# The first routing of a macaron block: a shorter product chain, earlier row stores, later expert weights, and another source of ones

## The chip, the cores and the metric

The kernel runs on one core of a Trainium2 chip. The metric is the device time of one execution in microseconds (us). The core has five engines that work beside each other and meet only at semaphores: TensorE (PE, matrix products and transposes), VectorE (DVE), ScalarE (ACT), GpSimd (POOL) and SyncE (SP, which here only issues transfers). Transfers are carried out by 16 DMA engines, whichever engine issued them. TensorE's clock has two levels, 2.4 and 1.2 GHz; the profile gives the granted clock as a share of the higher one.

## The reference

The input x is 4 batches of 512 tokens with 128 values each. The reference computes a "macaron" block of three residual steps:

```
x = x + 0.5 * ffn(layernorm(x))          # 8 experts, each token goes to one (top 1)
x = x + attention_block(layernorm(x))    # linear attention, then a quantised feed-forward net
x = x + 0.5 * ffn(layernorm(x))          # the same 8 experts again

def ffn(x):                              # W1: 8 x 128 x 512, W2: 8 x 512 x 128
    probs = softmax(x @ router_W + router_b)
    top1  = argmax(probs)
    h = relu(x @ W1[e] + b1[e]); y = h @ W2[e] + b2[e]
    return probs[top1] * y[top1]
```

The change lies in the first of the three steps, and in one preparation for the third.

## The kernel before

**Tiling.** The 2,048 tokens are 16 tiles of 128 rows, four to a batch. The first step sorts tokens by expert: every token gets a rank within its expert, every expert gets whole tiles of 128 slots, and 23 tiles (NT) are enough for any routing. The normalised rows are written to a scratch tensor in HBM (xn_scratch). For each slot tile the kernel gathers 128 rows from there by an indirect transfer, loads the expert's first weights and biases, and does the two layers. The second expert layer reads its weights W2 directly from the buffer that holds all eight experts.

**First routing.** Each engine has its own program.
- SyncE issues the loads of x (four), the router bias, the expert biases, all of W1 (2 MB), and then W2 of five experts (`load_w2`, five loads of 256 KB, in 512-byte pieces). Then it waits for the list of tile codes (`whole_ready`), reads it, and issues the loads of each tile's weights; from the second tile on it waits for the first gather too.
- VectorE makes the means and variances batch by batch. It then picks each token's expert in two halves (`pick(0, 0, 2)` and `pick(0, 2, 2)`, L1330), and between these makes a shift (minus mean times reciprocal deviation, `first_shift`) for each batch. The shift of batch 3 comes after the second pick. Then `route` (L1381) copies the hits, takes the tile counts, the ranks, the tile codes, and writes the source list srcu for the gathers.
- GpSimd makes constants in a fixed order, each raising `const_ready` by one: 7 is the step selectors, 8 the step column add_step, 9 rowid, 10 tileid, 11 and 12 token numbers, 13 and 14 the head masks. Among them it makes the reciprocal deviations (`first_rstd`). After 12 it writes all four tiles of batch 2's normalised rows (L582), then three tiles of row hits, then the masks, and a few small fills. Then it waits for the four row stores and for srcu and issues the gathers (L610). During gathers 10 to 13 it also fills xn with ones, a quarter at a time.
- ScalarE copies the transposed rows, writes the normalised rows of batches 0, 1 and 3 (`renormalise`, L775, each waits for its shift), and stores all four batches (`store_xn`, L782), batch 2 last, since GpSimd writes that one. Later it loads W2 of the last three experts.
- TensorE transposes x, makes the logits, and then in `ranks` (L977) and `tile_list` (L1011) the ranks and the tile table, as sums of products with masks. Products that are done only to keep the clock up are called warm products (`keep_warm(n)`, L927: each 512 columns of bf16). After the first routing's `sources` come eleven of them, and then the experts.

**Third step.** Its rows go to another scratch tensor, row_scratch, which has to hold ones wherever no token lands. SyncE fills it during attention: it waits until xn is full of ones (`fill_ready`) and until the last rows of the first step are back, then writes 9.2 MB from xn in nine transfers, each raising `fill_done`. GpSimd waits for `fill_done` before it scatters rows there. The buffer actT holds the looked-up activations of two batches; its half 1 is first written by the look-up of batch 1 (`lookup`, L861) on ScalarE.

Of the kernel before, what the change touches and what calls it, by code (L numbers as in the profile page):

```python
# [5 lines left out]
P = 128  # L6
D = 128
B = 4
S = 512
TOK = B * S  # L10
T = TOK // P
# [27 lines left out]
FILL = CODES * P * PW // P  # L39
UNROLL = 8  # L40
# [6 lines left out]
FILL_AT, FILL_PARTS = 10, 4  # L47
ROWS_BY_ACT = 4
ROWS_BY_POOL = 3
POOL_ROWS = 2  # L50
W2_BY_ACT = 3
# [14 lines left out]
def macaron_kernel(nc, x_d, g1_d, b1_d, wq_d, wk_d, wv_d, wo_d, g2_d, b2_d, w1_d, w2_d,  # L66
# [18 lines left out]
    with ctx:  # L85
        def sb(name, shape, dt=f32):
            return ctx.enter_context(nc.sbuf_tensor(name, shape, dt))
# [113 lines left out]
        actT = sb("actT", [P, 2, FC, S])  # L201

# [199 lines left out]
        def _(sp):  # L402
# [5 lines left out]
            sp.dma_start(ew[:, :, W1_AT:W1_AT + F], ew1_d.rearrange("e p f -> p e f")).then_inc(ew_in, 16)  # L408
            load_w2(sp, range(NE - W2_BY_ACT))
# [33 lines left out]
            sp.wait_ge(fill_ready, FILL_PARTS)  # L443
            sp.wait_ge(yb_in[NG - 1], 16 * GT)
            for at in range(0, FILL, T * D):
                n = min(T * D, FILL - at)
                sp.dma_start(row_fill_v[:, at:at + n], xn[:, :, :].rearrange("p t d -> p (t d)")[:, 0:n]).then_inc(fill_done, 16)
# [25 lines left out]
        def _(pool):  # L473
# [92 lines left out]
            step_selectors()  # L566
# [4 lines left out]
            at.then_inc(const_ready, 1)  # L571
            g.iota(rowid[:, :], [[1, P]], base=0, channel_multiplier=0,
# [7 lines left out]

            for t in range(POOL_ROWS * GT, (POOL_ROWS + 1) * GT):
                last = g.tensor_scalar(xn[:, t, :], x[:, t, :], mv[:, t, 0:1], rstd[:, t, 0:1], ALU.subtract, ALU.mult)  # L582
            last.then_inc(xn_by_pool, 1)

# [5 lines left out]
            for m_, pat in ((bmask[:, :, :], [[-DH, H], [0, DH]]), (hmask[:, :], [[-DH, H]])):  # L590
                link(g.affine_select(out=m_, in_=m_, compare_op=ALU.is_ge, fill=0.0, base=0,
                                     pattern=pat, channel_multiplier=1))
                g.affine_select(out=m_, in_=m_, compare_op=ALU.is_ge, fill=0.0, base=DH - 1,
                                pattern=[[-s_, n_] for s_, n_ in pat], channel_multiplier=-1).then_inc(const_ready, 1)
# [3 lines left out]
            g.memset(vx[:, :, :, D:D + 1], 1.0).then_inc(ones_ready, 1)  # L598

# [7 lines left out]
            def move_rows():  # L607

                def gather(k):
                    g.indirect_dma_start(out=Xg[:, k % UNROLL, :], out_offset=None, in_=xn_scr,  # L610
                                         in_offset=bass.IndirectOffsetOnAxis(ap=srcu[:, k:k + 1], axis=0)
                                         ).then_inc(g_in[k % UNROLL], 16)

                for b in range(NG):
                    pool.wait_ge(xn_stored[b], 16)
                pool.wait_ge(src_ready, 1)
                for k in range(NT):
                    if k >= UNPACED:
                        paced(k - UNPACED)
                    gather(k)  # L620
                    if FILL_AT <= k < FILL_AT + FILL_PARTS:
                        ts = slice((k - FILL_AT) * GT, (k - FILL_AT + 1) * GT)
                        g.memset(xn[:, ts, :], 1.0).then_inc(fill_ready, 1)
                pool.wait_ge(posu_ready, 1)
# [82 lines left out]
            pool.wait_ge(fill_done, 16 * len(range(0, FILL, T * D)))  # L707
# [9 lines left out]
        def _(act):  # L717
# [57 lines left out]
            def renormalise(g):  # L775

                act.wait_ge(shift_ready, g + 1)
                for t in range(g * GT, (g + 1) * GT):
                    last = A(xn[:, t, :], x[:, t, :], ACT.Identity, scale=rstd[:, t, 0:1], bias=shift[:, t, 0:1])
                last.then_inc(xn_ready, 1)  # L780

            def store_xn(g):  # L782
                if g == POOL_ROWS:
                    act.wait_ge(xn_by_pool, 1)
                else:
                    act.wait_ge(xn_ready, 1 + g - (g > POOL_ROWS))
                act.dma_start(xn_scr_v[:, g, :, :], xn[:, g * GT:(g + 1) * GT, :]).then_inc(xn_stored[g], 16)
# [22 lines left out]
            store_xn(3)  # L810
            store_xn(POOL_ROWS)
# [49 lines left out]
            def lookup(b, chunks=range(FC)):  # L861
                for c in chunks:
# [58 lines left out]
        def _(pe):  # L921
# [55 lines left out]
            def ranks():  # L977
# [3 lines left out]
                pe.wait_ge(const_ready, 10)  # L981
                mm(bank[5][0:NV, 0:1], whole[:, :], ones_v[0:1, 0:1], start=True, stop=False, skip_group_check=True)
                mm(bank[5][0:NV, 2:4], ident[0:NV, 0:NV], add_step[:, :], start=False, stop=False, skip_group_check=True)
# [10 lines left out]
                keep_warm(1)  # L994
# [3 lines left out]
                mm(bank[6][:, 0:NT], ones_v[0:1, :], tileid[0:1, :], start=True, stop=False, skip_group_check=True)  # L998
# [12 lines left out]
            def tile_list():  # L1011

                pe.wait_ge(tcol_ready, 1)
# [4 lines left out]
                keep_warm(1)  # L1018
# [136 lines left out]
            keep_warm(11)  # L1155
# [149 lines left out]
        def _(dve):  # L1305
# [63 lines left out]
            def first_shift(g):  # L1369

                ts = slice(g * GT, (g + 1) * GT)
                dve.wait_ge(rstd_ready, g + 1)
# [217 lines left out]
            first_shift(2)  # L1590
# [4 lines left out]
            first_shift(3)  # L1595
# [175 lines left out]
```

## Time and profile before

| | us |
|---|---|
| median of 3 runs | 207.23 |
| lowest, highest | 206.13, 208.17 |
| the profiled execution's own time | 205.5 |
| its span, first to last instruction | 203.8 |

| engine | busy us | share of the span |
|---|---|---|
| PE matmul | 187.3 | 92% |
| PE weight load | 158.8 | 78% |
| DVE | 122.3 | 60% |
| ACT | 111.8 | 55% |
| POOL | 122.2 | 60% |

The profile is of one execution; starts are counted from the beginning of its span. Busy time on TensorE includes the modelled end of each product and the warm products, so a busy TensorE isn't one that does useful work. L and a number is a line of the kernel. In a timeline a row may stand for several like instructions (x4), and the brackets at its end give the idle time before it and what ended that. "issue" is time in which the engine waited for nothing that the profile shows. The run is about 1.7 us longer than the span.

### The profile page before, as it was taken

To read this page: it belongs to the slowest core of one execution; us is meant where nothing else is said; L and a number is where in the kernel's file an instruction comes from. 1 tells how busy PE (TensorE), PEld (TensorE's weight loads), DVE (VectorE), ACT (ScalarE), POOL (GpSimd) and SP (SyncE) were. 2 spreads that over 40 slices of the span, in tenths; PEclk is the share of its full clock that TensorE was granted. 3 is DMA by queue.
4 is the path that set the end of the run, shared out by engine and by line. 5 is a ranking of instruction groups with operands and counts; after the bars stand their busy time and mean duration, and the time that the engine had idled before them with its cause. 6 is when DMAs were issued, how large, how long until landed. Compare 5 with 4: busy or idle time off the path is not lost.

```text
span 203.8 us, 4562 instructions
## 1 busy us (share of the span) xinstructions
PE 187.3 (92%) x1410; PEld 158.8 (78%) x1410; DVE 122.3 (60%) x518; ACT 111.8 (55%) x326; POOL 122.2 (60%) x186
## 2 busy tenths in 40 slices
PE   4999769999999978998999999989998999999992
PEld 2985349899999966786865869679635999999991
DVE  4767511222222887898897584867515677777762
ACT  2457225566556648787969853401302766766770
POOL 6886675697773676371787540847771344544554
PEclk9965599999999999999999999999999999999998
DMA  5999759867798561399991000011037868674800
GB/s 200 226 378 357 252 185 375 286 213 245 204 199 296 140 177 45 132 413 428 413 411 52 2 3 0 30 42 44 30 122 247 286 237 281 225 266 156 274 28 0
DMA packets 26680, 40.26 MB, mean 198 GB/s; under 512 B 4229, under 2 KB 16296, under 8 KB 25632
## 3 DMA queue, kind: packets, MB, share of 16 engines
q1 hardware_dynamic: 21136, 33.01, 46.1%
q0 software_dynamic: 2496, 4.76, 9.1%
q10 hardware_dynamic: 3024, 2.20, 3.4%
q8 instruction: 12, 0.20, 0.4%
q14 instruction: 12, 0.10, 0.1%
HBM read 10.78 MB, written 14.46 MB: 124 GB/s over the span
## 4 chain that ended last, share of the span: by engine, by line
PE 67%; DVE 11%; DMA 10%; issue 4%; POOL 3%; ACT 2%; ACTq 1%; SPq 0%; POOLq 0%; DVEq 0%
PE bank L1102 18%; PE bank L1119 17%; PE bank L1238 7%; PE bank L1254 6%; DMA Xg<-xn_scratch,srcu 4%; PE bank L927 3%; PE bank L974 3%; PE bank L1095 3%; DMA xn_scratch<-xn 2%; DMA eqrq<-row_scratch 2%; PE bank L943 2%; PE bank L1179 2%; DMA w<-in_L_attn_w_dram 2%; PE bank L1193 2%; PE bank L1203 1%
## 5 line engine op out<-in xcount | busy, mean ns | idle before, releaser
L748 ACT ACTIVATE hT<-bank,ewc_own 128x128 f32<-128x128 f32 x184 | 52.5, 369 | 48.3 <-PE bank L1102 48.2
L1102 PE MATMUL bank<-xT,ewc_own 128*128 128x128 f32 x368 | 48.8, 276 | 0.4 <-DVE xT L1455 0.3
L1119 PE MATMUL bank<-ew,hT 128*128 x368 | 48.5, 275 | 0.0
L1102 PEld LDWEIGHTS bank<-xT,ewc_own 128*128 128x128 f32 x368 | 44.7, 192 | 1.2 <-issue 1.2
L1119 PEld LDWEIGHTS bank<-ew,hT 128*128 128x128 f32 x368 | 44.7, 192 | 0.2 <-issue 0.2
L682 POOL DMA_INDIRECT out_dram<-ysb,eqrq x23 | 22.6, 983 | 25.4 <-DVE ysb L1465 25.1
L610 POOL DMA_INDIRECT Xg<-xn_scratch,srcu x23 | 22.0, 958 | 10.6 <-issue 5.8
L927 PE MATMUL bank<-ones_bf 128*128 128x512 bf16 x66 | 21.1, 451 | 3.9 <-POOL ident L500 2.7
L674 POOL DMA_INDIRECT row_scratch<-pay,posu x16 | 15.8, 988 | 10.8 <-DVE posu L1428 7.1
L1461 DVE TENSOR_TENSOR ysb<-bank,ewc_own 128x128 f32<-128x128 f32 x23 | 6.7, 289 | 26.0 <-PE bank L1119 26.0
L635 POOL DMA_INDIRECT xnT<-slot_scratch,posu x16 | 15.9, 997 | 9.4 <-DMA slot_scratch<-ysb 3.1
L1455 DVE COPY xT<-bank 128x128 f32<-128x128 f32 x46 | 13.0, 283 | 7.0 <-PE bank L1095 7.0
L1254 PE MATMUL bank<-w,actT 128*128 128x128 f32 x128 | 16.3, 278 | 0.0
L927 PEld LDWEIGHTS bank<-ones_bf 128*128 128x128 bf16 x66 | 6.8, 114 | 11.2 <-issue 4.3
L1095 PE MATMUL bank<-ident,Xg 128*128 128x128 f32 x46 | 12.9, 281 | 2.7 <-DMA Xg<-xn_scratch,srcu 1.9
L1254 PEld LDWEIGHTS bank<-w,actT 128*128 128x128 f32 x128 | 15.1, 192 | 0.0
L1238 PE MATMUL bank<-h1T,w 128*128 128x512 f32 x32 | 14.4, 592 | 0.0
L1465 DVE SCALAR_TENSOR_TENSOR ysb<-bank,gate,ysb 128x128 f32<-128x128 f32 x23 | 8.1, 351 | 10.3 <-PE bank L1119 10.1
L864 ACT ACTIVATE actT<-ewc_own 128x512 f32<-128x512 int16 x16 | 9.3, 621 | 8.0 <-DVE ewc_own L1666 8.0
L1474 DVE TENSOR_SCALAR Xg<-eqrq 128x128 f32<-128x128 f32 x23 | 7.8, 340 | 4.8 <-DMA eqrq<-row_scratch 4.6
L1238 PEld LDWEIGHTS bank<-h1T,w 128*128 128x128 f32 x32 | 5.8, 190 | 5.7 <-issue 5.5
L1666 DVE TENSOR_SCALAR ewc_own<-bank 128x512 int16<-128x512 f32 x16 | 10.0, 682 | 0.1
(240 smaller groups left out, 305.8 us busy)
## 6 DMA issues: line engine op xcount, KB each, us to landing
ewc_own<-ew SPq DMA_DIRECT2D x46, 322.0 KB, 3.1
row_scratch<-xn SPq DMA_DIRECT2D x8, 1024.0 KB, 10.6
ew<-in_L_ffn_W_dram SPq DMA_DIRECT2D x1, 2048.0 KB, 10.8
slot_scratch<-ysb SPq DMA_DIRECT2D x23, 64.0 KB, 1.8
ew<-in_L_ffn_W_dram SPq DMA_DIRECT2D x5, 256.0 KB, 8.7
eqrq<-row_scratch SPq DMA_DIRECT2D x18, 70.0 KB, 2.4
x<-in_L_attn_x_dram SPq DMA_DIRECT2D x4, 256.0 KB, 3.5
xn_scratch<-xn ACTq DMA_DIRECT2D x4, 256.0 KB, 5.7
```

What stands on the lines that cost most here:

```text
L610: g.indirect_dma_start(out=Xg[:, k % UNROLL, :], out_offset=None, in_=xn_scr, in_offset=bass.IndirectOffsetOnAxis(ap=srcu[:, k:k + 1], axis=0)
L635: g.indirect_dma_start(out=Yg[:, t, :], out_offset=None, in_=slot_scr[0:UPTO[group] * P, :], in_offset=bass.IndirectOffsetOnAxis(ap=posu[: ...
L674: g.indirect_dma_start(out=row_scr, out_offset=bass.IndirectOffsetOnAxis(ap=posu1[:, t:t + 1], axis=0), in_=pay[:, t, :], in_offset=None). ...
L682: g.indirect_dma_start(out=out_rows, in_=ysb[:, k, :], in_offset=None, bounds_check=TOK - 1, oob_is_err=False, out_offset=bass.IndirectOff ...
L748: last = A(hT[:, t.slot, c * P:(c + 1) * P], up_bank(k, c)[:, c * P:(c + 1) * P], ACT.Relu, scale=0.5 if m else 1.0, bias=ewc[t.ahead][:, ...
L927: mm(bank[2][:, :], ones_bf[:, :], bc(ones_bf[:, :].unsqueeze(1), [P, 4, P]), start=True, stop=True)
L1095: nc.tensor.transpose(bank[t.parity][:, 0:P], Xg[:, t.ahead, :], ident[:, :]).then_inc(xg_T, 1)
L1102: last = mm(up_bank(k, c)[:, c * P:(c + 1) * P], ewc[t.ahead][:, c * P:(c + 1) * P], xT[:, t.slot, :], start=True, stop=True)
L1119: last = mm(bank[4 + t.parity][:, 0:D], hT[:, t.slot, c * P:(c + 1) * P], ew[:, bass.ds(e[k], 1), W2_AT + c * D:W2_AT + (c + 1) * D].squee ...
L1238: mm(hidden_bank(c)[:, :], w1[:, c * P:(c + 1) * P], h1T[:, b % 2, :], start=True, stop=True).then_inc(u_ps, 1)
L1254: last = mm(row_bank(b, j)[:, j * P:(j + 1) * P], actT[:, b % 2, c, j * P:(j + 1) * P], w2[:, c, :], start=c == 0, stop=c == FC - 1)
L1455: v.tensor_copy(xT[:, t.slot, :], bank[t.parity][:, 0:P]).then_inc(xT_ready, 1)
```

## The change

- `ranks` waits for six constants where it waited for ten. The product that starts the step columns with add_step stands behind the wait for the second pick, where the product with the tile numbers stood; the latter moves into `tile_list`, in place of a warm product. The warm product in `ranks` is taken out. The eleven warm products before the experts are seven.
- GpSimd writes two of batch 2's four row tiles, before the remaining constants; ScalarE writes the other two. add_step comes before the step selectors (so it is 7 and they are 8). The head masks come before the row hits.
- The shifts of batches 2 and 3 are one VectorE instruction, between the picks.
- SyncE waits until ScalarE has written the rows of three batches (`xn_ready`, 3) before it issues W2's five loads.
- The ones for row_scratch are in a buffer of their own, 128 rows of 512 values that lie in the last quarter of actT's half 1; each transfer reads them repeatedly. There are ten transfers in place of nine. The fills of xn between the gathers are gone, one fill stands before the gathers, and ScalarE waits for `fill_done` before the look-up of batch 1.

```diff
 # SyncE
+            sp.wait_ge(xn_ready, NG - 1)
             load_w2(sp, range(NE - W2_BY_ACT))
 ...
-            sp.wait_ge(fill_ready, FILL_PARTS)
+            sp.wait_ge(fill_ready, 1)
             sp.wait_ge(yb_in[NG - 1], 16 * GT)
             for at in range(0, FILL, T * D):
                 n = min(T * D, FILL - at)
-                sp.dma_start(row_fill_v[:, at:at + n], xn[:, :, :].rearrange("p t d -> p (t d)")[:, 0:n]).then_inc(fill_done, 16)
+                whole_cols = n // FILL_COLS * FILL_COLS
+                sp.dma_start(row_fill_v[:, at:at + whole_cols].rearrange("p (a c) -> p a c", c=FILL_COLS),
+                             bc(filler.unsqueeze(1), [P, n // FILL_COLS, FILL_COLS])).then_inc(fill_done, 16)
+                if whole_cols < n:
+                    sp.dma_start(row_fill_v[:, at + whole_cols:at + n], filler[:, 0:n - whole_cols]).then_inc(fill_done, 16)
 # GpSimd
             for n in range(NG):
                 first_rstd(n)
-            step_selectors()
+            pool.wait_ge(rstd_ready, POOL_ROWS + 1)
+            for t in range(POOL_ROWS * GT + HALF_ROWS, (POOL_ROWS + 1) * GT):
+                last = g.tensor_scalar(xn[:, t, :], x[:, t, :], mv[:, t, 0:1], rstd[:, t, 0:1], ALU.subtract, ALU.mult)
+            last.then_inc(xn_by_pool, 1)
 ...                                  (add_step, const_ready 7)
+            step_selectors()
 ...                                  (rowid, tileid, the token numbers; the four rows stood here;
 ...                                  the head masks now stand here, then the row hits)
             g.memset(vx[:, :, :, D:D + 1], 1.0).then_inc(ones_ready, 1)
+            g.memset(filler, 1.0).then_inc(fill_ready, 1)
 ...
                     gather(k)
-                    if FILL_AT <= k < FILL_AT + FILL_PARTS:
-                        ts = slice((k - FILL_AT) * GT, (k - FILL_AT + 1) * GT)
-                        g.memset(xn[:, ts, :], 1.0).then_inc(fill_ready, 1)
 # ScalarE
-                act.wait_ge(shift_ready, g + 1)
-                for t in range(g * GT, (g + 1) * GT):
+                act.wait_ge(shift_ready, min(g, POOL_ROWS) + 1)
+                for t in range(g * GT, g * GT + HALF_ROWS if g == POOL_ROWS else (g + 1) * GT):
 ...
             store_xn(3)
+            renormalise(POOL_ROWS)
             store_xn(POOL_ROWS)
 ...
             def lookup(b, chunks=range(FC)):
+                if b == 1 and chunks[0] == 0:
+                    act.wait_ge(fill_done, 16 * FILLS)
 # TensorE
                 pe.wait_ge(oh_ready, picks(0, 0))
-                pe.wait_ge(const_ready, 10)
-                mm(bank[5][0:NV, 0:1], whole[:, :], ones_v[0:1, 0:1], start=True, stop=False, skip_group_check=True)
-                mm(bank[5][0:NV, 2:4], ident[0:NV, 0:NV], add_step[:, :], start=False, stop=False, skip_group_check=True)
+                pe.wait_ge(const_ready, 6)
 ...
-                keep_warm(1)
+                mm(bank[5][0:NV, 0:1], whole[:, :], ones_v[0:1, 0:1], start=True, stop=False, skip_group_check=True)
                 pe.wait_ge(oh_ready, picks(0))
                 mm(bank[4][:, 4:5], oh[:, :, :].rearrange("p t e -> p (t e)"), ones_bf[:, 0:1], start=True, stop=True
                    ).then_inc(hits_ps, 1)
-                mm(bank[6][:, 0:NT], ones_v[0:1, :], tileid[0:1, :], start=True, stop=False, skip_group_check=True)
+                pe.wait_ge(const_ready, 7)
+                mm(bank[5][0:NV, 2:4], ident[0:NV, 0:NV], add_step[:, :], start=False, stop=False, skip_group_check=True)
 ...                                  (in tile_list)
+                pe.wait_ge(const_ready, 8)
                 pe.wait_ge(tcol_ready, 1)
 ...
-                keep_warm(1)
+                pe.wait_ge(const_ready, 10)
+                mm(bank[6][:, 0:NT], ones_v[0:1, :], tileid[0:1, :], start=True, stop=False, skip_group_check=True)
                 pe.wait_ge(inv_ready, 1)
 ...
-            keep_warm(11)
+            keep_warm(7)
 # VectorE
             pick(0, 0, 2)
-            first_shift(2)
+            first_shift(2, 2)
 ...
             pick(0, 2, 2)
-            first_shift(3)
```

## Rows read from the trace of the kernel before

**Rows 1.** Chain of waits, 10 to 40 us; start us, us, what.

```profile
17.69 4.64 DMA xn_scratch<-xn
...
23.75 1.25 POOL Xg L610
...
26.55 3.30 DMA Xg<-xn_scratch,srcu
...
30.23 0.92 PE bank L1102 x8
...
31.88 4.33 DMA Xg<-xn_scratch,srcu
```

**Rows 2.** Timeline of VectorE: start, us, line, operation, out<-in, shapes [idle before].

```profile
13.56 0.23 DVE L1337 TENSOR_TENSOR lg<-bank,rstd 128x64 f32<-128x64 f32 x1 [0.87 <-PE bank L974]
...
14.33 0.43 DVE L1343 TENSOR_TENSOR lg<-lg,lmax 128x64 f32<-128x64 f32 x1
...
15.91 0.16 DVE L1387 COPY hits<-bank 128x1 f32<-128x1 f32 x1 [0.30 <-PE bank L996]
...
22.50 0.18 DVE L1379 TENSOR_SCALAR srcu<-bank 128x23 uint32<-128x23 f32 x1 [1.09 <-PE bank L1077]
```

**Rows 3.** Timeline of TensorE's products, 10 to 30 us.

```profile
10.63 2.89 PE L974 MATMUL bank<-rwc,xnT 128*128 128x8 f32 x16
...
13.58 0.24 PE L983 MATMUL bank<-add_step,ident 32*32 32x2 f32 x2
...
15.71 0.61 PE L998 MATMUL bank<-tileid,ones_v 1*128 1x23 f32 x2
...
16.50 0.27 PE L1005 MATMUL bank<-hits,sums 128*32 128x1 f32 x2
...
17.31 0.61 PE L927 MATMUL bank<-ones_bf 128*128 128x512 bf16 x1
...
18.46 2.31 PE L927 MATMUL bank<-ones_bf 128*128 128x512 bf16 x5
...
22.31 3.88 PE L927 MATMUL bank<-ones_bf 128*128 128x512 bf16 x11
26.52 0.33 PE L1095 MATMUL bank<-ident,Xg 128*128 128x128 f32 x1 [0.33 <-DMA Xg<-xn_scratch,srcu]
...
29.90 0.33 PE L1095 MATMUL bank<-ident,Xg 128*128 128x128 f32 x1 [1.14 <-DMA Xg<-xn_scratch,srcu]
```

**Rows 4.** Timeline of GpSimd: rows, row hits, and a fill between the gathers.

```profile
13.44 3.14 POOL L582 TENSOR_SCALAR xn<-x,mv,rstd 128x128 f32<-128x128 f32 x4
18.45 2.49 POOL L587 TENSOR_SCALAR inr<-rowid,rf,token 128x128 f16<-128x128 f16 x3 [1.88 <-DVE rf L1402]
...
40.41 0.54 POOL L623 MEMSET xn<- 128x512 f32 x1
```

**Rows 5.** Timeline of ScalarE: the rows of batch 3.

```profile
15.64 1.65 ACT L779 ACTIVATE xn<-x,shift,rstd 128x128 f32<-128x128 f32 x4 [2.42 <-DVE shift L1373]
```

**Rows 6.** Timeline of SyncE's queue, 4 to 33 us.

```profile
4.72 10.11 SPq L371 DMA_DIRECT2D ew<-in_L_ffn_W_dram  x5
21.51 11.10 SPq L417 DMA_DIRECT2D ewc_own<-ew  x8
```

**Rows 7.** Stretches: length, busy us (instructions) by engine, granted clock, DMA share, GB/s.

```profile
11.00:12.00 1.00, 1.00 (x9) 1.00 (x8) 0.90 (x4) 1.00 (x4) 0.68 (x3) 0.71 1.04 401
...
20.00:25.00 5.00, 3.90 (x25) 1.47 (x24) 3.42 (x13) 1.41 (x4) 3.60 (x10) 0.50 0.87 279
25.00:30.00 5.00, 3.20 (x18) 1.66 (x16) 0.58 (x2) 1.14 (x4) 3.79 (x4) 0.99 0.50 172
```

**Rows 8.** Timeline of SyncE's queue: the writes of row_scratch.

```profile
84.56 9.56 SPq L447 DMA_DIRECT2D row_scratch<-xn  x9
```

**Rows 9.** Stretches: the end of these writes.

```profile
105.00:110.00 5.00, 4.75 (x24) 3.03 (x23) 3.60 (x9) 4.67 (x10) 4.57 (x10) 1.00 0.52 214
```

**Rows 10.** Timeline of ScalarE: the first look-ups of batch 1.

```profile
115.21 1.13 ACT L864 ACTIVATE actT<-ewc_own 128x512 f32<-128x512 int16 x2
```

More of the change, by code:

```diff
@@ L39 @@
 FILL = CODES * P * PW // P
+FILL_COLS = S
+FILLS = FILL // (T * D) + (FILL % (T * D) >= FILL_COLS) + (FILL % FILL_COLS > 0)
 UNROLL = 8
@@ L46 @@
 DEEP = 4
-FILL_AT, FILL_PARTS = 10, 4
 ROWS_BY_ACT = 4
@@ L50 @@
 POOL_ROWS = 2
+HALF_ROWS = GT // 2
 W2_BY_ACT = 3
@@ L201, in macaron_kernel @@
         actT = sb("actT", [P, 2, FC, S])
+        filler = actT[:, 1, FC - 1, :]
         ewc = [ewc_own[:, u, :] for u in range(UNROLL)]
@@ L579, in _ @@
                    channel_multiplier=-GT, allow_small_or_imprecise_dtypes=True).then_inc(const_ready, 1)
-            for t in range(POOL_ROWS * GT, (POOL_ROWS + 1) * GT):
-                last = g.tensor_scalar(xn[:, t, :], x[:, t, :], mv[:, t, 0:1], rstd[:, t, 0:1], ALU.subtract, ALU.mult)
-            last.then_inc(xn_by_pool, 1)
-            pool.wait_ge(rf_ready, 1)
-            for t in range(T - ROWS_BY_ACT - ROWS_BY_POOL, T - ROWS_BY_ACT):
-                g.tensor_scalar(inr[:, t, :], rowid[:, :], rf[:, t:t + 1], token1[:, t:t + 1], ALU.is_equal, ALU.mult
-                                ).then_inc(inr_by_pool, 1)
             for m_, pat in ((bmask[:, :, :], [[-DH, H], [0, DH]]), (hmask[:, :], [[-DH, H]])):
@@ L594, in _ @@
                                 pattern=[[-s_, n_] for s_, n_ in pat], channel_multiplier=-1).then_inc(const_ready, 1)
+            pool.wait_ge(rf_ready, 1)
+            for t in range(T - ROWS_BY_ACT - ROWS_BY_POOL, T - ROWS_BY_ACT):
+                g.tensor_scalar(inr[:, t, :], rowid[:, :], rf[:, t:t + 1], token1[:, t:t + 1], ALU.is_equal, ALU.mult
+                                ).then_inc(inr_by_pool, 1)
             g.memset(pay[:, :, TOK_AT + 1:LG_AT], 0.0).then_inc(pay_ready, 1)
@@ L706, in _ @@
             residuals(B - 1)
-            pool.wait_ge(fill_done, 16 * len(range(0, FILL, T * D)))
+            pool.wait_ge(fill_done, 16 * FILLS)
             for b in range(1, B):
@@ L784, in store_xn @@
                     act.wait_ge(xn_by_pool, 1)
-                else:
-                    act.wait_ge(xn_ready, 1 + g - (g > POOL_ROWS))
+                act.wait_ge(xn_ready, (1, 2, 4, 3)[g])
                 act.dma_start(xn_scr_v[:, g, :, :], xn[:, g * GT:(g + 1) * GT, :]).then_inc(xn_stored[g], 16)
@@ L1367, in row_hits, with first_shift @@
                                     ALU.is_equal, ALU.mult).then_inc(inr_ready, 1)
-            def first_shift(g):
-                ts = slice(g * GT, (g + 1) * GT)
-                dve.wait_ge(rstd_ready, g + 1)
+            def first_shift(g, n=1):
+                ts = slice(g * GT, (g + n) * GT)
+                dve.wait_ge(rstd_ready, g + n)
                 v.scalar_tensor_tensor(out=shift[:, ts, 0:1], in0=rstd[:, ts, 0:1], scalar=-1.0, in1=mv[:, ts, 0:1],
```

## The prediction

> **What bounds the kernel now.** I read the chain of waits first. Between the first routing and the first expert it leaves the engines: the store of a batch's normalised rows is under way from 17.69 us for 4.64 us, so lands at 22.33, and GpSimd's first gather begins at 23.75 [rows 1]. Then I read VectorE's timeline for the other thing that the gather waits for: the source list, written at 22.50 in 0.18 us, so there at 22.68 [rows 2]. The two releasers lie 0.35 us apart, and the later one is the list. Whatever frees the stores alone is worth nothing in this execution; what moves the list is worth its full length until the stores are last.
>
> TensorE's timeline shows what the list hangs on and what cover there is. The 16 logits products hold the engine from 10.63 to 13.52. The hits product goes once the last pick is done, then the tile-number product at 15.71 takes 0.61, and only at 16.50 comes the count product, for which everything in VectorE's routing waits [rows 3]. VectorE had its copy of the hits at 15.91 + 0.16 = 16.07 [rows 2]: TensorE, not VectorE, is late there. The first expert's rows are turned at 26.52, and at 29.90, after 1.14 us of idle time, the third tile's [rows 3]. From there TensorE runs with few gaps, so a shift at the third gather goes through to the end, save what a later wait eats.
>
> **The change part by part.**
>
> *Products moved in the ranks.* The tile-number product (0.61) leaves the stretch between hits and counts, and the step product (0.24) comes in [rows 3]. 0.61 - 0.24 = 0.37 us. The count product would start at 16.13, just behind the hits copy's end at 16.07, so no more than 0.43 can be had here, and 0.37 is taken. The tile-number product now stands where a warm product of the same 0.61 stood, at 17.31: nothing. The warm product taken out of the ranks lay before the wait for the second pick: nothing. The waits for constants themselves cost nothing before: logits held the engine until 13.52 and GpSimd had left its constants at 13.44 [rows 4]. All of VectorE's routing, the five warm products at 18.46 [rows 3], TensorE's reading of the list and the source products follow in chain, so the list comes at 22.31.
>
> *GpSimd's order.* Two rows instead of four are written, and before the constants rather than after: 3.14 / 4 = 0.79 each, so the constants end at 13.44 + 1.57 = 15.01 at the latest [rows 4]. The first that is awaited after a pick is needed at about 15.7, the tile numbers at 16.9: 0.7 us of cover or more. The masks move ahead of the row hits; they and the small fills filled at most 20.94 to 23.75, 2.81 us, so they end by 17.8, and the row hits are released at 18.45 - 0.37 = 18.08 [rows 4]. Behind the hits (2.49) comes the new fill of ones, 128x512, at 0.54, as the four taken out of the gathers [rows 4]: 18.08 + 2.49 + 0.54 = 21.1, plus the small fills, under the 22.31 of the list. Cover gone, it would cost 0.54. The four fills taken out stood beside a TensorE that had its tiles: nothing.
>
> *Rows and stores on ScalarE.* It sat idle 2.42 us, from 13.22 on, for the last shift before batch 3's four rows at 15.64 (1.65 us, to 17.29) [rows 5]; the store was under way 0.40 later, at 17.69 [rows 1]. The shift of both batches is now made before the second pick. The rows begin at 13.22, or 13.6 behind the issue of the store before them, and are done by 15.3; the store is under way at 15.7 and lands, with the old 4.64 us, at 20.3. Two rows of batch 2 (0.83) and its store follow: under way at about 16.9, landed at 21.6. Worth nothing by itself, since the list is last; it keeps the stores from being last.
>
> *Second weights.* Five loads, which SyncE issued from 4.72 to 14.83 at 2.0 us each [rows 6], wait for three batches of rows, about 15.3. They are beside the last two stores, not behind them: the wait counts rows written, not stores landed. An issue takes 0.4 where the queue is free (the store's) and, in the burst of eight tile loads with waits in it, at most 11.10 / 8 = 1.4 [rows 1, 5, 6]. Five take 2 to 7 us, so SyncE is free at 17.3 to 22.3; behind them it has the list to read and its first tile load, which stood at 21.51. The weights themselves are wanted by the first down product, behind the 0.92 of the second up that begins at 30.23 [rows 1]: cover enough. Price 0, with up to +0.5 if the first tile load comes over a microsecond late.
>
> *The gathers' landings.* The DMA engines now have the second weights to move while the first gather lands. How much that costs no row shows; it is bounded by the nearest landings. The first turn came 2.77 us after its gather's start; the third landed in 3.30, the sixth, in a crowd, in 4.33 [rows 1, 3]. A first landing of 4.33 would be 1.6 later, of which 1.14 is idle time before the third. A third landing of 4.33 would be a straight +1.03. Less traffic could also give up to -0.5. I take 0, since the crowd should be gone by the time of the third.
>
> *Warm products.* Eleven at 22.31 become seven. They take up to 0.46 each at the lower clock (2.31 / 5), so 3.2 us, ending at 25.2, before the first rows at 26.2: nothing, if the clock is kept.
>
> *VectorE beside GpSimd.* One of the second pick's steps took 0.43 at 14.33, where its neighbour took 0.23 [rows 2]. GpSimd then read and wrote rows [rows 4]. The Trainium skill, SBUF — State Buffer, "SBUF: two separate sides", says that a VectorE instruction with two SBUF inputs and a GpSimd one that reads SBUF exclude each other for a whole instruction. By that rule the rows in their new place would hold up the first pick instead, by up to 0.79 a step, and the trace agrees only in part: one step of several was held, by 0.21. Without the rule: the second pick may gain 0.21 and the first may lose it several times over, but VectorE then sat idle for 0.87 us until the logits were out [rows 2]. Price 0, bounds -0.21 and +0.5.
>
> *The fill of the row scratch.* Nine writes become ten, from one row of 512 ones read again and again. Issued from 84.56 [rows 8], they keep the DMA engines full to about 107.6 (share 0.52 of 105 to 110) [rows 9]. ScalarE must now wait for them before the second batch's look-up at 115.21 [rows 10]. Some 7.6 us of cover on 23 of traffic: it would have to run a third slower to matter. Nothing.
>
> **Sum.** The profiled execution took 205.5 us, its span 203.8 and 1.7 around it. 205.5 - 0.37 = 205.1. The median of the runs shown is 207.23, 1.7 above the profiled one, for reasons that no row tells; with that offset kept, **206.8 us**.
>
> **The rivals.**
> - *Stores were late in the other executions* (0.25). With only 0.35 us between stores and list, an execution with slower stores waits for the stores, and the change takes them out of the way by 1.3 to 2 us. Then the median gains its 1.7 of offset in good part too: 207.23 - 0.37 - 1.4 = 205.4. For: the traffic at that point and the runs' spread of 2 us. Against: nothing shows where the spread comes from.
> - *The clock goes* (0.20), the one that ends slower. Place: the end of the seven warm products. The granted clock was 0.50 over 20 to 25 us and 0.99 over 25 to 30; the five products at 18.46 had not raised it, the sources and the eleven had. It fell at 11 to 12 us with TensorE busy throughout [rows 7]. With four products fewer, TensorE does nothing from about 25.2 to 26.2, and the clock may not rise, or may fall before the third tile. The up and the down products of a tile, 0.92 us each at the full clock [rows 1], then take 1.8: the sixth gather waits for an up, +0.9 at once, up to +1.9 and once more if it lasts. 207.23 - 0.37 + 1.5 = 208.4, to 206.9 + 3.8 = 210.7. It decides as soon as the granted clock is 0.5 at 26 us or later. Against: over 25 to 30 TensorE was busy only 3.20 of 5.00 and kept the clock. The Trainium skill (TensorE: Matmul & The Clock Gate, "What's actually happening") has the clock lowered only after a stretch of idleness; by that rule this rival would be nearly nil, and the sum stands. The fall at 11 to 12 with no idle time disagrees, so I keep its chance.
> - *Second weights in the gathers' way* (0.12): the third landing at 4.33, or a late first tile load: 207.23 - 0.37 + 1.0 = 207.9.
> - *The change doesn't do what it says* (0.08): the count product starts no earlier, because the second pick or the step selectors are late. 207.2.
>
> **How the numbers follow.** My forecast has 0.35. About 1%, 2.07 us, is what a measurement of this kernel can tell from no change. Under 205.16 lie half of the first rival and a fifth of the forecast: 0.20. Above 209.3 lie two fifths of the clock rival and a quarter of the crowd (where it delays several landings): 0.11. Within: 0.69. The range takes in the first rival on one side and the clock's single price on the other: 205.0 to 208.9.
>
> **What would show it.** Right: the count product near 16.1; the source list's write near 22.1; GpSimd's first gather near 23.4; row stores landed by 21.5; third turn near 29.5; clock 1.0 from 25 us. Wrong: the first gather still at 23.7 with VectorE's list unmoved; a granted clock of 0.5 after 26 us; a gather that takes over 4 us before the third turn; ScalarE waiting for the fill near 115 us.

## The result, and the profile after

The changed kernel is slower: 207.53 us against 205.98, both medians of 20 runs; ratio 1.0069, 95% interval 1.0045 to 1.0093, so about +1.4 us. The ratio leaves out executions in a slower state, four of the changed kernel's 20, one of them of 273.35 us. I had forecast 206.8 from a median of 207.23, a gain of 0.4. That 207.53 lies in my range of 205.0 to 208.9 is luck: the range was laid around the median of three runs, 207.23, which 20 runs put at 205.98, and the time moved the other way. The profiled execution has a span of 206.5 us, before 203.8.

The chain of waits of the changed kernel, 10 to 45 us (start us, us, what):

```profile
15.99 3.80 DMA xn_scratch<-xn
...
20.11 0.43 POOL actT L608
20.54 1.91 issue
22.45 0.04 POOLq L626
22.49 0.84 issue
23.34 4.46 DMA Xg<-xn_scratch,srcu
...
28.86 2.05 PE bank L1112 x8
...
31.60 1.97 PE bank L1112 x8
33.57 0.89 PE bank L1129 x8
```

Read it against [rows 1]. The first gather starts 0.41 us earlier (23.34, was 23.75), but takes 4.46 us to land. The two first-layer products behind it ("ups", L1112; the second layer's are "downs", L1129) take 2.0 us each, where they took 0.9 to 1.1. The first down starts at 33.57; before, the second up ended at 31.15 and the down followed. The loss is made between 23 and 34 us.

VectorE and TensorE in their timelines, as in [rows 2, 3]:

```profile
11.60 0.25 DVE L1363 TENSOR_TENSOR oh<-key,kmax 128x64 bf16<-128x64 f32 x1
...
15.08 0.16 DVE L1397 COPY hits<-bank 128x1 f32<-128x1 f32 x1 [1.38 <-POOL token L589]
...
21.65 0.18 DVE L1389 TENSOR_SCALAR srcu<-bank 128x23 uint32<-128x23 f32 x1 [1.07 <-PE bank L1087]
```

```profile
13.76 0.19 PE L1003 MATMUL bank<-ones_bf,oh 128*128 128x1 bf16 x1 [1.01 <-DVE oh L1363]
...
15.38 0.24 PE L1013 MATMUL bank<-hits,sums 128*32 128x1 f32 x2 [0.99 <-DVE hits L1397]
...
21.46 3.15 PE L936 MATMUL bank<-ones_bf 128*128 128x512 bf16 x7
27.84 0.47 PE L1105 MATMUL bank<-ident,Xg 128*128 128x128 f32 x1 [3.23 <-DMA Xg<-xn_scratch,srcu]
...
28.86 2.05 PE L1112 MATMUL bank<-xT,ewc_own 128*128 128x128 f32 x8
```

The source list came at 21.83, 0.85 us earlier than before. A part of it is the clock, which was high during the logits in this execution (below). GpSimd had finished its fill at 20.54 and the list was there at 21.83, yet its wait ended at 22.49. The stores were what it waited for: their landings took 3.6 to 6.4 us, and batch 2's, issued at 15.99, with 6.4 lands at 22.4. TensorE then sat idle for 3.23 us before the first turn.

This holds for the kernel before too, and I had read it otherwise. Its chain, and the time from issue to landing of its last two stores (issued at 17.32 and 17.69):

```profile
17.69 4.64 DMA xn_scratch<-xn
22.33 0.10 POOL pay L596
...
22.48 0.38 issue
22.86 0.04 POOLq L616
...
DMA to landing us min/median/max: 4.8/5.0/5.1
```

The 4.64 us end where a small fill of GpSimd's takes over in the chain, not where the store lands. Batch 2's, issued at 17.69, lands 5.1 us later, at 22.8, behind the list of 22.68, and GpSimd's wait ends at 22.86. So the stores were the last already, by some 0.1 us. They now land 0.4 us earlier, and the first gather starts 0.41 us earlier; the list's 0.85 us show nowhere.

VectorE's copy of the hits shows something that I hadn't priced: 1.38 us of idle time, ended by GpSimd's token numbers. TensorE had the hits at 13.95. The constants, now behind two rows, had become the late ones.

Stretches of both kernels, first before, then after (length, busy us by engine, granted clock, DMA share, GB/s):

```profile
14.00:17.00 3.00, 2.65 (x24) 1.89 (x23) 1.74 (x9) 1.35 (x4) 2.57 (x4) 0.50 1.14 344
...
23.00:25.00 2.00, 2.00 (x6) 0.76 (x5) 1.51 (x6) 0.00 (x0) 1.25 (x1) 0.50 0.87 282
25.00:28.00 3.00, 2.34 (x13) 1.08 (x11) 0.29 (x1) 0.00 (x0) 2.09 (x3) 0.99 0.21 61
```

```profile
14.00:17.00 3.00, 1.91 (x20) 1.65 (x19) 1.34 (x7) 1.75 (x5) 2.09 (x10) 0.50 0.85 295
...
23.00:25.00 2.00, 1.61 (x4) 0.30 (x2) 0.69 (x4) 0.00 (x0) 1.37 (x2) 0.50 1.13 310
25.00:28.00 3.00, 0.16 (x1) 0.16 (x2) 0.00 (x0) 0.00 (x0) 2.39 (x3) 0.50 0.29 85
```

Over 14 to 17 us the DMA engines' share is 0.85 where it was 1.14: W1 runs out, and W2, issued from 14.58 on, comes too late. I call this the hole. The work left undone comes back at 23 to 25 us (0.87 becomes 1.13), under the first gather. Over 25 to 28 us TensorE is busy for 0.16 us, and its clock, which stood at 0.99 before, stays at 0.50, the lower of its two levels, until within 30 to 35 us (0.66 there; before 1.00).

### The profile page after: what moved, and what is told of

The parts are those of the page before. It is cut to its first block, busy times and chain, and to the rows that moved or that the text cites. A ratio compares the mean times of both kernels' runs of the same rounds, so it can differ in the third digit from the quotient of the medians.

```text
span 206.5 us, 4550 instructions
## 1 busy us (share of the span) xinstructions
PE 185.6 (90%) x1404; PEld 157.9 (76%) x1404; DVE 122.2 (59%) x517; ACT 112.7 (55%) x328; POOL 119.0 (58%) x181
## 4 chain that ended last, share of the span: by engine, by line
PE 61%; DVE 11%; DMA 10%; POOL 6%; issue 5%; ACT 4%; SPq 1%; ACTq 0%; POOLq 0%; DVEq 0%
PE bank L1112 19%; PE bank L1129 16%; PE bank L1248 7%; PE bank L1264 5%; POOL row_scratch L681 3%; ACT xn L786 3%; PE bank L1105 2%; DMA Xg<-xn_scratch,srcu 2%; DMA ewc_own<-ew 2%; DMA row_scratch<-pay,posu 2%; PE bank L1189 2%; DMA xn_scratch<-xn 2%; DMA w<-in_L_attn_w_dram 2%; PE bank L952 2%; PE bank L1203 2%
## 5 line engine op out<-in xcount | busy, mean ns | idle before, releaser
L1112 PE MATMUL bank<-xT,ewc_own 128*128 128x128 f32 x368 | 50.6, 282 | 1.3 <-DMA ewc_own<-ew 0.9
L1112 PEld LDWEIGHTS bank<-xT,ewc_own 128*128 128x128 f32 x368 | 46.3, 198 | 3.1 <-issue 1.9
L1129 PE MATMUL bank<-ew,hT 128*128 x368 | 48.5, 275 | 0.0
L1129 PEld LDWEIGHTS bank<-ew,hT 128*128 128x128 f32 x368 | 44.8, 192 | 0.2 <-issue 0.2
L936 PE MATMUL bank<-ones_bf 128*128 128x512 bf16 x60 | 19.2, 454 | 3.8 <-POOL ident L509 2.7
L1264 PEld LDWEIGHTS bank<-w,actT 128*128 128x128 f32 x128 | 15.1, 192 | 0.0
L936 PEld LDWEIGHTS bank<-ones_bf 128*128 128x128 bf16 x60 | 6.1, 114 | 10.4 <-issue 3.9
L1105 PEld LDWEIGHTS bank<-ident,Xg 128*128 128x128 f32 x46 | 6.8, 148 | 5.5 <-DMA Xg<-xn_scratch,srcu 4.1
```

The lines of the kernel that those rows point to most:

```text
L936: mm(bank[2][:, :], ones_bf[:, :], bc(ones_bf[:, :].unsqueeze(1), [P, 4, P]), start=True, stop=True)
L1105: nc.tensor.transpose(bank[t.parity][:, 0:P], Xg[:, t.ahead, :], ident[:, :]).then_inc(xg_T, 1)
L1112: last = mm(up_bank(k, c)[:, c * P:(c + 1) * P], ewc[t.ahead][:, c * P:(c + 1) * P], xT[:, t.slot, :], start=True, stop=True)
L1129: last = mm(bank[4 + t.parity][:, 0:D], hT[:, t.slot, c * P:(c + 1) * P], ew[:, bass.ds(e[k], 1), W2_AT + c * D:W2_AT + (c + 1) * D].squee ...
L1264: last = mm(row_bank(b, j)[:, j * P:(j + 1) * P], actT[:, b % 2, c, j * P:(j + 1) * P], w2[:, c, :], start=c == 0, stop=c == FC - 1)
```

## The experiments

A profile is one execution and the ratio rests on many, so the last two columns of the table tell the mechanism and not the size. All ratios are to the kernel before, with 95% intervals. "First gather" is the time from its start to what it released, in the chain, or else from the timelines to the first turn. The column of W2 says how many of the five loads are issued behind SyncE's wait. Three profiles lie at the edge of their runs: e3's and e5's are of the fastest execution (204.06 and 205.11 us), e12's of the slowest (207.50, median 205.76).

| kernel | W2 behind | warm | ratio | first gather us | first down at us |
|---|---|---|---|---|---|
| before | 0 | 11 | 1 | 2.8 | 31.0 |
| changed | 5 | 7 | 1.0069 (1.0045, 1.0093) | 4.5 | 33.4 |
| e1 | 5 | 11 | 1.0085 (1.0044, 1.0126) | 5.2 | 33.9 |
| e9 | 5 | 20 | 1.0058 (1.0020, 1.0096) | 5.1 | 32.6 |
| e2 | 0 | 7 | 1.0040 (1.0004, 1.0076) | 2.8 | 31.8 |
| e11 | 5, wait one batch earlier | 7 | 1.0029 (0.9993, 1.0066) | 3.2 | 31.2 |
| e12 | 5, wait one batch earlier | 11 | 0.9989 (0.9959, 1.0019) | 3.1 | 32.3 |
| e3 | 0 | 11 | 0.9980 (0.9941, 1.0018) | 3.7 | 30.3 |
| e6 | 3 | 11 | 0.9976 (0.9937, 1.0015) | 3.0 | 31.1 |

**e1, e2, e3: undo the warm products, the wait, both.**

```diff
-            keep_warm(7)
+            keep_warm(11)        # e1, e3
-            sp.wait_ge(xn_ready, NG - 1)      # e2, e3
```

> The changed kernel with eleven warm products before the experts, as before, in place of seven. Clock theory (the cost is TensorE's clock, which stayed at the lower level through the first two ups because too few warm products stood before them): the granted clock is 1.0 by the first up, the ups take 0.9 us instead of 2.0, and the ratio to the kernel before falls from 1.007 to 0.998 to 1.002. Traffic theory (the cost is the first gather, which landed 4.5 us after its start because the second weights were moved at that time): the first turn stays near 27.8 us and the ratio stays at 1.005 to 1.009.

> The changed kernel without SyncE's wait: the second weights of five experts are issued at once, as before; seven warm products stay. Traffic theory: the first gather lands in 2.7 us again, the first turn stands near 25.9, and the ratio is 0.996 to 1.000. Clock theory: the gap before the first turn gets shorter, but seven warm products may still not bring the clock, so the ups stay slow in some executions: ratio 1.000 to 1.005.

> Both undone: no wait of SyncE, eleven warm products. What is left of the change is the shorter product chain, the rows split over two engines and the buffer of ones. Clock and traffic theories together: 0.994 to 0.998, since the source list came 0.85 us earlier in the changed kernel. If the cost lay elsewhere (in the buffer of ones or the new wait of ScalarE): 1.004 or more.

In e1 four warm products given back change nothing (1.0085). That alone doesn't clear the clock: it did rise behind them, but was lost again before the first up, so only e9 below tests it.

```profile
21.82 3.91 PE L936 MATMUL bank<-ones_bf 128*128 128x512 bf16 x11
28.31 0.47 PE L1105 MATMUL bank<-ident,Xg 128*128 128x128 f32 x1 [2.59 <-DMA Xg<-xn_scratch,srcu]
28.58 0.63 PE L936 MATMUL bank<-ones_bf 128*128 128x512 bf16 x1
29.33 2.05 PE L1112 MATMUL bank<-xT,ewc_own 128*128 128x128 f32 x8
```

Eleven products in 3.91 us are 0.36 apiece, against 0.46 in [rows 3] at the lower level: the last of them ran high (granted clock 1.00 over 25 to 28 us, 0.51 over 28 to 30). Between them and the up of 2.05 lie 2.59 us of waiting. Its hole is deeper than the changed kernel's (share 0.53 over 14 to 17, as in e9, 0.52), and its first gather slower, 5.2 us against 4.5. e2 takes the wait away: the first gather lands in 2.8 us, and of the 0.69% some 0.3 go. With seven warm products the ups are still slow (2.05 and 2.04), though the gather is not late: seven are too few by themselves. e3 does both and is at 0.998, clear of the changed kernel's 1.0069, so what it undoes is the whole loss. In its profile the up takes 1.13 us, and its span is 202.3:

```profile
26.27 0.33 PE L1104 MATMUL bank<-ident,Xg 128*128 128x128 f32 x1 [1.44 <-DMA Xg<-xn_scratch,srcu]
26.44 0.38 PE L935 MATMUL bank<-ones_bf 128*128 128x512 bf16 x1
27.15 1.13 PE L1111 MATMUL bank<-xT,ewc_own 128*128 128x128 f32 x8 [0.33 <-DVE xT L1464]
```

**e4: seven warm products in the kernel before.**

```diff
-            keep_warm(11)
+            keep_warm(7)
```

> The kernel before with seven warm products in place of eleven, nothing else. Clock theory: four warm products fewer alone lose the clock in some or all executions, ratio 1.003 to 1.010. Traffic theory: the first gather lands as before, so the gap behind seven warm products is short and nothing changes, 0.999 to 1.001.

0.9994 (0.9955 to 1.0032). Its profile lost the clock all the same (ups of 2.05 and 1.68 us, first down at 31.52, 0.56 later than before), and no time shows. So the lost clock alone is worth less than the 1 to 2 us that I gave it. The first up's delay fills idle time that TensorE has anyway before the third turn [rows 3]: the second up starts at 30.01, where it started at 30.06. A later wait takes most of the rest: the sixth turn is at 36.40, before at 36.25.

**e9: enough warm products to bridge the late gather.**

```diff
-            keep_warm(7)
+            keep_warm(20)
```

> The changed kernel with twenty warm products in place of seven, so that TensorE is at work until the late first gather has landed. If the slow ups are the larger part of the loss: clock 1.0 at the first up, the first down near 31.3 instead of 33.4, ratio 0.998 to 1.003. If the late gather is: the ratio stays at 1.005 or more, for the gathers behind it come late as well.

The clock was kept (an up of 1.13 us at 29.66) and the ratio is still 1.0058: with the gather at 5.1 us the first down comes at 32.6. So the larger part of the loss is the late gather. Its chain shows how that reaches the first down:

```profile
23.68 5.06 DMA Xg<-xn_scratch,srcu
28.74 0.02 issue
28.76 0.21 SPq L422
28.97 0.04 issue
29.02 2.52 DMA ewc_own<-ew
31.53 0.04 issue
31.58 1.17 PE bank L1112 x8
```

SyncE waits for the first gather before it loads the second tile's weights, and these take another 2.5 us; the second up waits for them. I had priced the first gather by the turn behind it alone.

**e5 and e10: the product chain alone; the chain undone.**

```diff
 # e5: on the kernel before, the edits of ranks and tile_list, and add_step ahead of step_selectors
 # e10: on e3
-                pe.wait_ge(const_ready, 6)
+                pe.wait_ge(const_ready, 7)
+                mm(bank[5][0:NV, 0:1], whole[:, :], ones_v[0:1, 0:1], ...)
+                mm(bank[5][0:NV, 2:4], ident[0:NV, 0:NV], add_step[:, :], ...)
 ...
+                pe.wait_ge(const_ready, 10)
+                mm(bank[6][:, 0:NT], ones_v[0:1, :], tileid[0:1, :], ...)   # between hits and counts again
```

> The kernel before with the shorter product chain alone (and the step column made before the step selectors, as it needs): no other part of the change. My sum gave it 0.37 us: count product right behind the hits copy, ratio 0.997 to 0.999. If the list was not what the gather waited for in most executions, because the row stores landed later, the list comes earlier and the time does not move: 0.999 to 1.001.

> The changed kernel without SyncE's wait, with eleven warm products and with the old product chain (tile numbers between hits and counts, both warm products); rows on two engines, early stores and buffer of ones stay. Beside the same kernel with the short chain (0.998): if the chain is worth its 0.4 us here, 1.000 to 1.002; if the DMA engines and not the list set when the first gather lands, no difference: 0.997 to 0.999.

e5 was at 1.0050 (1.0012 to 1.0087), outside both expectations. Its list was written at 21.08, its stores landed at 21.94, and they, not the list, released the gather:

```profile
16.56 5.38 DMA xn_scratch<-xn
21.94 0.03 POOLq L615
...
22.89 3.89 DMA Xg<-xn_scratch,srcu
```

So the 0.37 us of my sum was not there to be had. Why it was slower than before is open, and the profile, of its fastest execution, can't tell much: its first gather took 3.9 us, and an earlier list also brings the first tile load and ScalarE's W2 loads forward, under that gather, but I did not separate these. e10, 0.9998 (0.9965 to 1.0031), beside e3's 0.9980: the difference is the 0.4 us of my sum, but the intervals overlap, and the chain is worth nothing that I can measure. In e10's profile, where the stores are early and the chain long, it is the list that comes last (written at 22.35, the last store landed at 21.6), so with early stores a shorter chain may be worth something; that isn't shown.

**e6: two W2 loads ahead of the wait, three behind.**

```diff
+            load_w2(sp, range(2))
             sp.wait_ge(xn_ready, NG - 1)
-            load_w2(sp, range(NE - W2_BY_ACT))
+            load_w2(sp, range(2, NE - W2_BY_ACT))
```

> The changed kernel with eleven warm products, and two of the five second-weight loads issued before SyncE's wait, three behind it. Traffic theory: the cost goes with the bytes that are moved under the first gather, so the first gather lands between the 2.7 us of no load behind the wait and the 5.2 of five, and the ratio lies between 0.998 (none) and 1.0085 (five): about 1.000 to 1.005. If the wait itself, SyncE being late with the first tile load, were the cost, the ratio would stay at 1.006 or more.

0.9976 (0.9937 to 1.0015), with eleven warm products, as e1, which had 1.0085. The wait stayed in the same place; only the queue was no longer empty while SyncE waited. I had expected an effect in proportion to the bytes behind the wait; with three it is gone, and so is the hole:

```profile
14.00:17.00 3.00, 2.21 (x27) 1.80 (x25) 1.91 (x10) 2.07 (x6) 1.90 (x10) 0.50 1.10 354
```

**e11, e12: the wait one batch earlier.**

```diff
-            sp.wait_ge(xn_ready, NG - 1)
+            sp.wait_ge(xn_ready, NG - 2)
-            keep_warm(7)
+            keep_warm(11)        # e12
```

> The changed kernel with SyncE waiting for two batches of rows instead of three, seven warm products. Theory of the hole: in the changed kernel the DMA engines ran dry at 14 to 17 us (share 0.65 at 15 to 16) because the first weights were through before the second were issued, and those 1.5 us of traffic came back on top of the first gather. With the wait over at 12.5 to 13 us the second weights follow the first ones without a gap: share over 1.0 throughout, first gather lands in 2.7 to 3.7 us, ratio as without the wait, 1.001 to 1.005 with the clock still lost. Theory of order (anything that moves the second weights behind the stores loses): 1.006 or more.

> The same with eleven warm products. Theory of the hole: as the kernel without wait and with eleven, 0.996 to 1.000, clock 1.0 at the first up. Theory of order: as the changed kernel with eleven, 1.005 to 1.009.

All five loads are still behind a wait, but it is over before W1 is through. The hole is gone in both; e12's rows:

```profile
14.00:17.00 3.00, 2.28 (x21) 2.01 (x21) 1.44 (x8) 2.10 (x6) 1.95 (x10) 0.50 1.07 354
...
23.00:25.00 2.00, 2.00 (x7) 0.65 (x5) 0.32 (x2) 0.00 (x0) 1.25 (x1) 0.70 0.88 259
```

(Share 1.07 where the changed kernel has 0.85, and 0.88 at 23 to 25 where it has 1.13; e11 has 1.08 and 0.73.) The ratios are 1.0029 and 0.9989, against 1.0069 and 1.0085 with the hole and the same warm products. With eleven warm products the intervals are apart, and the hole is shown as the cause of that loss; with seven, the changed kernel's own number, they overlap. One expectation failed: the clock of e12's profile, the slowest of its executions, was granted and lost again (0.93 over 25 to 28 us, 0.50 over 28 to 30; ups of 2.04).

**e8, e13, e14: take traffic away from under the first gather.**

```diff
 # e8: no wait; SyncE's five loads stand behind the first three tile loads; eleven warm products
+                if k == FIRST:
+                    load_w2(sp, range(NE - W2_BY_ACT))
 # e13 on e3, e14 on e6
+            act.wait_ge(g_in[0], 16)
             load_w2(act, range(NE - W2_BY_ACT, NE))
```

> The changed kernel with eleven warm products and the five second-weight loads issued only behind the first three tile loads, so after the first gather has landed. Traffic theory: the row stores land before 20 us, the first gather lands in 2.7 us or less and the first turn stands at 26 or earlier, with the clock at 1.0; the first down product then has to wait for its weights to 32 to 34 us, so the ratio is 1.005 to 1.02 all the same. Clock theory without traffic: the first turn stays near 28.

> The kernel without SyncE's wait and with eleven warm products (0.998), and ScalarE's three second-weight loads, 768 KB that moved at 20 to 25 us beside the first gather, issued only once the first gather has landed. Traffic theory: less under the first gather and the first tile load, first gather lands in 2.2 to 2.8 us instead of 3.65, first turn up to 1 us earlier, ratio 0.993 to 0.998, unless the three loads now hold up the second and third gathers by as much. If traffic under the first gather is not what counts: 0.997 to 1.001, or 1.003 and more if the first down product waits for its weights.

> The kernel with two second-weight loads ahead of SyncE's wait and three behind it (0.9976), with the same delay of ScalarE's three. Traffic theory: as before it, 0.993 to 0.998; the best of all if both hold. Otherwise 0.997 to 1.003.

All three land the first gather in 2.8 us, as the traffic theory says, and all three lose, e8 and e14 more than I had expected: 1.0363 (1.0280 to 1.0446), 1.0318 (1.0247 to 1.0390), 1.0180 (1.0109 to 1.0251). They rest on three or four executions each. e13's engines are nearly empty while the first gather lands, and full for the third:

```profile
23.00:26.00 3.00, 2.15 (x9) 0.72 (x7) 0.32 (x2) 0.00 (x0) 2.40 (x3) 0.90 0.08 22
...
29.00:32.00 3.00, 0.86 (x4) 0.86 (x5) 0.29 (x1) 0.00 (x0) 0.12 (x1) 0.74 0.97 312
```

```profile
25.69 0.33 PE L1105 MATMUL bank<-ident,Xg 128*128 128x128 f32 x1 [0.85 <-DMA Xg<-xn_scratch,srcu]
...
31.14 0.47 PE L1105 MATMUL bank<-ident,Xg 128*128 128x128 f32 x1 [3.06 <-DMA Xg<-xn_scratch,srcu]
31.41 1.92 PE L1112 MATMUL bank<-xT,ewc_own 128*128 128x128 f32 x8
33.97 2.07 PE L1129 MATMUL bank<-ew,hT 128*128 x8 [0.64 <-DMA ew<-in_L_ffn_W_dram]
```

The first turn comes 0.6 us earlier than e3's, the third turn waits 3.06, the clock falls again, and the first down waits for its weights. In e8 it waits 5.6 us. Bytes moved away from under the first gather come back under a later one, or are missing at the first down.

**e7: the buffer of ones alone, on the kernel before.**

```diff
+            g.memset(filler, 1.0).then_inc(fill_ready, 1)
 ...
-                        g.memset(xn[:, ts, :], 1.0).then_inc(fill_ready, 1)
 ...                                  (the ten transfers and ScalarE's wait as in the change)
```

> The kernel before with the buffer of ones alone: ten transfers that read 2 KB of ones again and again, one fill before the gathers, ScalarE's wait for them before batch 1's look-up. My step priced it at nothing, with 7.6 us of cover: 0.998 to 1.002, ScalarE's wait over before the look-up. If the smaller pieces made the writes a third slower, ScalarE would wait near 115 us and the ratio be 1.003 or more.

0.9998 (0.9954 to 1.0041). It is the part of the change that was priced rightly, with less cover than I thought: see below. Its profile shows one more thing: the second up took 2.08 us and the first down came at 32.51. So the clock can be lost with eleven warm products and the old order of loads, too.

None of the fourteen beats the kernel before beyond its interval. e6, e3 and e12 come nearest.

## Why the prediction was wrong

- **Second weights: price 0.** This is the step that failed. I asked when the weights are due and whether SyncE is free, and it was (issues from 14.58 to 17.75 us). I did not ask what the DMA engines do while SyncE waits. W1 runs out, and W2 begins too late to fill the gap. e6 and e12 close the hole and the loss goes (0.9976, 0.9989, where e1 has 1.0085); e11 closes it with seven warm products and is at 1.0029.
- **The gathers' landings: price 0, bounds -0.5 and +1.6.** The same fault at its other end. The first turn came 4.50 us after its gather's start instead of 2.77, so 1.73 later, just above my upper bound. The crowd was gone by the third landing, as I said (share 0.29 over 25 to 28 us), but the first stood in it. The cover of 1.14 us before the third turn was not the right one either: the second tile's weights wait for the first gather too (e9).
- **Warm products: nothing, if the clock is kept.** The condition failed: the granted clock was 0.50 until 33 us. The rival *The clock goes* had this right. Seven warm products lose the clock also where the gather is not late (e2, e4), and a late gather loses it also behind eleven (e1). Its price of 1.5 us was wrong: in the kernel before the loss costs nothing that can be measured (e4). Seven or eleven makes 0.6% (e2, e3) and 0.4% (e11, e12) once the other parts are in. The intervals of each pair overlap.
- **Stores on ScalarE: landed at 20.3 and 21.6.** Issued earlier than computed (14.59 and 15.99). Batch 3's landed at 18.2, but batch 2's took 6.4 us beside W2 on the other queue, and came at 22.4. The old landing time was itself misread, 4.64 us for 5.1. My own remark that W2 goes beside the stores and not behind them had this in it, and I kept the old landing time.
- **Products: -0.37.** The list came early enough. It was worth nothing, since the stores came last, in the changed kernel and in e5. The prediction's premise was wrong: in the kernel before, too, the stores landed last, at 22.8, and the list was there 0.1 us ahead of them, not 0.35 us behind. "Whatever frees the stores alone is worth nothing" had it the wrong way round.
- **GpSimd's order: constants in time.** Wrong in this execution. I set the need at 15.7 us, from an execution in which the logits ran mostly at the lower clock. Here they ran high, the picks were done at 13.7, and VectorE waited for the token numbers until 15.1. The stores hid it.
- **VectorE beside GpSimd: 0.** The first pick was hardly held up by the rows: at most 0.28 us a step (L1359 at 11.04), 0.06 above the usual 0.22. The Trainium skill's rule (SBUF — State Buffer, "SBUF: two separate sides"), by which one waits for the other's whole instruction, would have allowed up to 0.79 more a step; the trace of the changed kernel doesn't show it.
- **The clock rule.** By the Trainium skill (TensorE: Matmul & The Clock Gate, "What's actually happening") the clock goes down after idleness. e1 agrees: the clock was granted, then lost with TensorE idle for 2.59 us. The changed kernel doesn't bear on it: its clock stood at 0.50 from 14 us on, so there was nothing to lose, and I had used a rule about the fall against a rival that was about the rise. The fall at 11 to 12 us with TensorE busy throughout [rows 7] still doesn't agree.
- **The fill: nothing.** Right, but the writes got slower. They end at about 111.8 (share 0.36 of 110 to 115) and the look-up starts at 116.92: the cover went from 7.6 to 5.1 us.
- **The offset of 1.7 us and the first rival.** Of the offset, 1.25 us came from having three runs (207.23, then 205.98 of 20). The rival's condition held, the stores were last, but the change took them only 0.4 us out of the way, and no gain shows.

In sum, of +1.4 us none is the chain's. By the middles of the intervals the hole costs 0.8 us with seven warm products (1.0069 - 1.0029) and 2.0 with eleven (1.0085 - 0.9989); without the hole, seven instead of eleven cost 0.8 (1.0029 - 0.9989, or 1.2 by e2 and e3). Only the 2.0 is clear of the noise, so how the +1.4 divides between hole and clock stays open. The second and third rivals, given 0.32 together, both happened, the third at the first gather and not at the third.

## What to carry to other kernels

Before a transfer is put behind a wait, look at what its queue holds meanwhile: where the DMA engines are full for long before the first consumer (here a share of 1.0 and more up to 20 us), a wait may change the order of transfers but should not let the engines run dry. It is made good by leaving a part ahead of the wait or by waiting for an earlier event. Two releasers a few tenths of a microsecond apart are one bound, and speeding up one is worth nothing until the other moves too. The end of a transfer in a chain of waits can be the point where the chain leaves it; compare it with the time from issue to landing. When a transfer is late, follow everything that waits for it, here also the next tile's weights. Durations and due times from one execution hold for its clock; check a constant's due time for the case that the clock is high as well.

## What the runs showed of the hardware

- The first 64 KB indirect gather lands 2.7 to 3.0 us after its start where the DMA engines' share is below 1 over 20 to 23 us (before, e2, e4, e7, e8, e13, e14), 3.0 to 3.9 where it is 1.04 to 1.16 there and below 1 over 23 to 25 (e3, e5, e6, e10, e11, e12), and 4.5 to 5.2 where it stays above 1.1 up to 25 us (changed, e1, e9).
- Writes of 9.2 MB to HBM in 2 KB pieces, which read the same row of ones again and again, go slower than in 8 KB pieces from xn. Which of the two differences it is, the runs don't tell. The first row is of the changed kernel, the second of the kernel before:

```profile
100.00:105.00 5.00, 4.75 (x37) 3.95 (x35) 4.52 (x16) 3.50 (x8) 4.56 (x9) 1.00 1.03 374
```

```profile
100.00:105.00 5.00, 4.55 (x35) 3.96 (x34) 4.60 (x23) 3.22 (x7) 4.67 (x9) 1.00 1.01 411
```

- TensorE's clock can be lost again after it has been granted: in e1 between eleven warm products and the first up, with 2.59 us of waiting between; in e12 there with 1.70; in e13 before the third tile.
